# Embedding, first normalisations and first v product run between the columns of the edge placing; groups go from PSUM to their places by ScalarE

## The reference, cut to what matters

```
h = max(layernorm(x), 0)                      # the first normalisation
# L0: 4 blocks of conditioned norm, attention over edges, MLP
emb  = concat(sin(noise * freqs), cos(noise * freqs))
cond = silu(emb @ f_w1 + f_b1) @ f_w2 + f_b2   # one row of 16 per node
for i in range(4):
    y = norm(x) * (1 + cond @ s1_w[i] + s1_b[i]) + cond @ b1_w[i] + b1_b[i]
    q, k, v = y @ wq[i] + bq[i], y @ wk[i] + bk[i], y @ wv[i] + bv[i]   # 4 heads of 128
    scores = (q[src] * k[dst]).sum(-1)
    ... softmax over the edges of one src, sum of attn * v[dst], @ wo[i] + bo[i]
    x = x + ...          # then a second conditioned norm and a relu MLP
# then L1 (one SAGE-like layer), L2 (two relational layers), L3 (two SAGE layers)
```

## Time and profile before

| | |
|---|---|
| median of 3 runs | 3067.86 us (3063.8 to 3068.15) |
| the profiled execution | 3068.89 us |
| its span (first to last instruction) | 3067.1 us |
| mean granted clock of TensorE | 0.972 of full |
| busy in the span | PE 2871.9, DVE 2059.3, ACT 810.1, POOL 765.6 us |

### The profile page before, as it was taken

The page is one execution under the profiler, slowest core; times in us unless marked ns, Lnnn a source line. Parts: engine busy times, 40 slices in busy tenths (PEclk is TensorE's granted clock), DMA queues, the critical chain, the costliest instruction groups (busy, mean ns, idle before and its releaser), DMA issues.

```text
span 3067.1 us, 31231 instructions
## 1 busy us (share of the span) xinstructions
PE 2871.9 (94%) x11230; PEld 1810.2 (59%) x11230; DVE 2059.3 (67%) x3698; ACT 810.1 (26%) x1152; POOL 765.6 (25%) x701
## 2 busy tenths in 40 slices
PE   5878899999999999999999999999999999999999
PEld 1245556676556666556667555667645566556555
DVE  9999856786757776756777765778787876623211
ACT  1154442223212222221222321222322213213221
POOL 5732403343023334022334130334410000000000
PEclk9989999999999999999999999999999999999999
DMA  3000110000300000310000220000245244421001
GB/s 83 17 8 1 42 55 1 1 28 30 125 21 14 1 28 14 117 45 14 1 28 1 86 90 14 1 28 1 69 124 153 66 130 141 127 82 38 14 0 34
DMA packets 74679, 143.61 MB, mean 47 GB/s; under 512 B 11429, under 2 KB 11820, under 8 KB 74525
## 3 DMA queue, kind: packets, MB, share of 16 engines
q1 hardware_dynamic: 68988, 129.58, 13.6%
q0 software_dynamic: 5536, 12.03, 1.2%
HBM read 130.66 MB, written 10.92 MB: 46 GB/s over the span
## 4 chain that ended last, share of the span: by engine, by line
PE 69%; DVE 21%; issue 5%; ACT 3%; DVEq 1%; DMA 1%; POOL 0%; POOLq 0%; SPq 0%
PE ps L1547 14%; PE ps L1777 11%; PE ps L1806 10%; PE ps L1658 6%; PE ps L1751 4%; PE ps L1538 4%; DVE prob L1025 4%; DVE x L1015 3%; PE ps L1500 2%; PE ps L1798 2%; PE ps L1564 2%; PE ps L1647 2%; PE ps L1632 2%; DVE ps L971 2%; DVE onehot_src L896 2%
## 5 line engine op out<-in xcount | busy, mean ns | idle before, releaser
L703 POOL TENSOR_TENSOR pacc<-pacc,prob 125x628 f32<-125x628 f32 (+1 forms) x288 | 405.3, 1407 | 348.9 <-DVE prob L1044 348.9
L1547 PE MATMUL ps<-yT,w 128*128 128x416 f32 (+1 forms) x1152 | 442.5, 541 | 18.5 <-DVE qk_lo L962 11.6
L1658 PE MATMUL ps<-prob,big 125*128 125x314 f32 x1280 | 393.8, 430 | 14.0 <-DVE prob L1044 10.7
L1366 ACT ACTIVATE prob<-prob 125x628 f32<-125x628 f32 x320 | 233.0, 728 | 572.8 <-DVE prob L1025 572.8
L1806 PE MATMUL ps<-pieces,counts_r 125*125 125x512 f32 x1400 | 355.8, 409 | 0.0
L1547 PEld LDWEIGHTS ps<-yT,w 128*128 128x128 f32 x1152 | 229.0, 201 | 206.8 <-issue 195.5
L1044 DVE SCALAR_TENSOR_TENSOR prob<-prob,typed 125x628 f32<-125x628 f32 x320 | 260.3, 813 | 70.4 <-ACT prob L1366 68.2
L1806 PEld LDWEIGHTS ps<-pieces,counts_r 125*125 125x125 f32 x1400 | 259.1, 187 | 77.6 <-issue 17.4
L1647 PE MATMUL ps<-qk_hi 128*125 128x314 f32 x640 | 270.1, 422 | 11.2 <-DVE prob L1025 10.6
L1658 PEld LDWEIGHTS ps<-prob,big 125*128 125x128 f32 x1280 | 227.6, 190 | 81.0 <-DVE prob L1044 27.2
L1025 DVE TENSOR_TENSOR prob<-ps,shift 125x628 f32<-125x628 f32 x320 | 257.3, 804 | 4.4 <-PE ps L1649 3.7
(11 more groups left out here) (213 smaller groups left out, 4411.2 us busy)
## 6 DMA issues: line engine op xcount, KB each, us to landing
basis<-in_basis SPq DMA_DIRECT2D x160, 256.0 KB, 2.7
lite_ring<-in_basis SPq DMA_DIRECT2D x120, 256.0 KB, 2.6
w<-in_m_w SPq DMA_DIRECT2D x8, 1024.0 KB, 6.7
w<-in_wk SPq DMA_DIRECT2D x5, 1024.0 KB, 6.7
w<-in_wv SPq DMA_DIRECT2D x4, 1024.0 KB, 5.6
w<-in_wq SPq DMA_DIRECT2D x4, 1024.0 KB, 5.4
oT<-in_cw SPq DMA_DIRECT2D x8, 512.0 KB, 3.8
w<-in_wo SPq DMA_DIRECT2D x4, 1024.0 KB, 5.4
```

The source lines that it names most:

```text
L703: nc.gpsimd.tensor_tensor(pacc[:, c0:c0 + nn], pacc[:, c0:c0 + nn], prob[:, n % 3, p0:p0 + nn], ALU.add).then_inc(psum_done, 1)
L1366: A.activation(prob[:, n % 3, :], prob[:, n % 3, :], ACT.Exp, scale=DH ** -0.5).then_inc(exp_done, 1)
L1547: last = mm(lin_ps(job, 128, nn), weight[:, k, m * 128:(m + 1) * 128], lhs[:, k, c0:c0 + nn], start=(k == 0), stop=(k == KD - 1))
L1658: last = mm(o_halves[:, b, :], vrow[:, t, h * DH:(h + 1) * DH], prob[:, n % 3, b * QUARTER:(b + 1) * QUARTER], start=(t == 0), stop=(t == ...
```

## The change

It moves work of block 0 ahead and takes another engine for the copies.

1. VectorE computes the phases ahead of the columns, and between columns: a tile's statistics behind each of columns 2, 4, ... 20, the low parts of the norm's matrices behind 14, the silu behind 25, the shifts behind 27, low parts of cond behind 34, 39, 44. From column 46 on, behind every eighth, one step of block 0's norm: statistics of tile n, scale of tile n - 2, addition of the bias to v of tile n - 5. TensorE has the counterpart: the hidden layer, cond, and per step a turn, a scale product and a v product. GpSimd's powers go between its one-hots.
2. In a group ScalarE reads the sum twice from PSUM, once to `run` and once to its place in `typed`, whose register it loads itself; VectorE makes `carry`. GpSimd takes no part. TensorE waits for `bucket_placed` before it reuses PSUM.
3. The first tile stage has no v product; behind tiles 2, 4, 6 and 8 (`TAKE_AT`) it has one of the first four products of head 1.
4. SyncE's loads stand in another order: noise and the embedding's weights, then x and wv, then the norm's matrices, the other weights and `att`, `gate_rows` last.

```diff
-PREP = (10, 20, 30)
-COND_AT = (40, 43, 46)
+STATS_AT, POWERS_AT, SHIFTS_AT = 2, 25, 27
+LOW_AT, HIDDEN_AT, SILU_AT = 14, 10, 25
+COND_AT, COND_LOW_AT = (30, 35, 40), (34, 39, 44)
+NORM_AT, NORM_EVERY = 46, 8
+TAKE_AT = (2, 4, 6, 8)
...
@@ VectorE
+            def first_norm_step(n):
+                if n < T:
+                    dve.wait_ge(x0_ready, n + 1)
+                    tile_statistics(n)
+                if 1 <= n <= T:
+                    tile_shift(0, n - 1)
+                if 2 <= n < T + 2:
+                    tile_scale(0, n - 2)
+                if 5 <= n < T + 5:
+                    if n == 5:
+                        dve.wait_ge(blkc_in, 32)
+                    add_v(first, n - 5)
...
+            first_phases()
             for c in range(EC):
...
+                n, rest = divmod(c - NORM_AT, NORM_EVERY)
+                if rest == 0 and n >= 0:
+                    first_norm_step(n)
...
             for g in range(GROUPS):
...
+                if g:
+                    if g >= 3:
+                        dve.wait_ge(group_full, g - 2)
+                    V.tensor_scalar(carry[:, g % 2, :], ident16[:], same[0:P, g - 1:g], None, ALU.mult).then_inc(carry_ready, 1)
...
-                if g == PREP[0]:
-                    first_norm()
-                if g == PREP[2]:
-                    finish_silu()
@@ ScalarE
+            norm(0)
             for g in range(GROUPS):
+                place = act.value_load(placei[0:1, g:g + 1], min_val=0, max_val=PLACE + (T - 1) * N)
                 act.wait_ge(*((group_full, g) if g else (onehot_used, STEPS)))
-                if g >= RUNS:
-                    act.wait_ge(bucket_placed, g - RUNS + 1)
                 A.activation(run[:, g % RUNS, :], ps[0:P, (g % 2) * 1536:(g % 2) * 1536 + N], ACT.Copy).then_inc(run_ready, 1)
-                if g + 1 < GROUPS:
-                    A.activation(carry[:, (g + 1) % 2, :], ident16[:], ACT.Copy, scale=same[0:P, g:g + 1]).then_inc(carry_ready, 1)
+                if g:
+                    A.drain()
+                A.activation(typed[:].bitcast(F16)[:, bass.ds(place, N)], ps[0:P, (g % 2) * 1536:(g % 2) * 1536 + N],
+                             ACT.Copy).then_inc(bucket_placed, 1)
@@ GpSimd
             for c in range(EC):
...
+                t = (c - NORM_AT - 3) // NORM_EVERY
+                if (c - NORM_AT - 3) % NORM_EVERY == 0 and 0 <= t < T:
+                    tile_power(t)
...
-            for g in range(GROUPS):
-                pool.wait_ge(run_ready, g + 1)
-                place = pool.value_load(placei[0:1, g:g + 1], min_val=0, max_val=(PLACE + (T - 1) * N) // 2)
...
@@ TensorE
+            def first_norm_step(n):
...
+                if 3 <= n < T + 3:
+                    norm_turn(0, n - 3)
+                if 1 <= n <= T:
+                    norm_scale(0, n - 1)
+                if 4 <= n < T + 4:
+                    t = n - 4
+                    if t == 0:
+                        pe.wait_ge(w_in[0], 16)
+                    pe.wait_ge(turned_ready, t + 1)
+                    row_product(first["v"][t], yT, t, w[0])
...
             for g in range(GROUPS):
                 if g >= 2:
-                    pe.wait_ge(run_ready, g - 1)
+                    pe.wait_ge(bucket_placed, g - 1)
...
+                    project(0)
+                    turn_counts(0)
+                    projected(0)
+                    for t in range(T):
+                        if t + 1 < T:
+                            turn_counts(t + 1)
+                        max_scores(0, 2 * t)
+                        max_scores(0, 2 * t + 1)
+                        if t in TAKE_AT:
+                            n = TAKE_AT.index(t)
+                            col_product(g["proj"][1][n], yT, n % 3, w[1 + n // 3], 1)
```

More of the change, by code:

```diff
@@ L81, in max_row @@
             g["mrow"][h] = [w.take() for _ in range(3)]
+    if first:
+        g["v"] = [w.take() for _ in range(T)]
     project(0)
-    g["v"] = [w.take() for _ in range(T)]
+    if not first:
+        g["v"] = [w.take() for _ in range(T)]
     project(1, 0)
@@ new lines, in _ @@
+            A.activation(typed[:].bitcast(F32), zcol[0:P, :].to_broadcast([P, PLACE]), ACT.Copy)
+            A.drain()
+            act.wait_ge(emb_ready, 1)
+            A.activation(emb, turns, ACT.Sin, scale=6.2831850)
+            A.drain().then_inc(emb_ready, 1)
+            act.wait_ge(stage_in, 16)
+            A.activation(cw[:, 0:2, :], stage, ACT.Copy).then_inc(cw_hi, 1)
+            for (c0, nn), job in zip(COLS, hj):
+                act.wait_ge(lin_full, job.full)
+                A.activation(z[:, c0:c0 + nn], lin_ps(job, COND, nn), ACT.Identity, bias=fb1[:]).then_inc(lin_empty[job.slot], 1)
@@ L1521, in _ @@
[L1521 to L1532 removed]
+            first = plan_block(walk, True)
@@ new lines, in _ @@
+            pe.wait_ge(turned_ready, T)
+            for g in range(GROUPS):
+                if g >= 2:
+                    pe.wait_ge(bucket_placed, g - 1)
+                for j in range(STEPS):
+                    n = g * STEPS + j
+                    pe.wait_ge(onehot_ready, n + 1)
+                    for c0, nn in WIDE:
+                        last = mm(ps[0:P, (g % 2) * 1536 + c0:(g % 2) * 1536 + c0 + nn], onehot_dst[:, g % 2, j, :],
+                                  onehot_src[:, n % 4, c0:c0 + nn], start=(j == 0), stop=(g == 0 and j == STEPS - 1))
+                    last.then_inc(onehot_used, 1)
+                if g:
+                    pe.wait_ge(carry_ready, g)
+                    pe.wait_ge(run_ready, g)
+                    for c0, nn in WIDE:
+                        last = mm(ps[0:P, (g % 2) * 1536 + c0:(g % 2) * 1536 + c0 + nn], carry[:, g % 2, :],
+                                  run[:, (g - 1) % RUNS, c0:c0 + nn], start=False, stop=True)
+                    last.then_inc(group_full, 1)
@@ new lines, in _, with turn_counts @@
+            pe.wait_ge(bucket_placed, GROUPS)
+            def turn_counts(s):
+                if s:
+                    pe.wait_ge(crow_copied, s)
+                dst_ps = o_ps[0:P, :].bitcast(F16)
+                for t in range(T):
+                    if s == 0:
+                        pe.wait_ge(ct_ready, t + 1)
+                    c0 = t * (P + 1) if t < 8 else 1024 + (t - 8) * (P + 1)
+                    last = nc.tensor.transpose(dst_ps[:, c0:c0 + P], ct[:, t, s * P:(s + 1) * P], ident16[:])
+                last.then_inc(crow_ps_full, 1)
@@ L1567, in norm_tiles, with col_product @@
+            def col_product(job, lhs, chunk, weight, m):
+                c0, nn = COLS[chunk]
+                reuse(job)
+                for k in range(KD):
+                    last = mm(lin_ps(job, 128, nn), weight[:, k, m * 128:(m + 1) * 128], lhs[:, k, c0:c0 + nn],
+                              start=(k == 0), stop=(k == KD - 1))
+                last.then_inc(lin_full, 1)
             def norm_tiles(k, update, product):
```

436 lines of the change are left out of this document (210 added, 226 removed).

## The result

The changed kernel takes 3078.64 us (median of 7 runs, 3075.99 to 3081.62) against 3067.86 (7 runs, 3063.80 to 3068.66): a ratio of 1.0038, 95% interval 1.0027 to 1.0049. It is slower by 10.8 us. The forecast, 3068.5, is missed by 10.1; the range of 3056 to 3092 holds the time.

A forecast was written before the change was run, and what follows sets the result against it. VectorE was taken to bound the groups, and with GpSimd the columns. Stage ends summed to -1.2 us at the exponentials, taken as +0.6 for optimistic hand-offs: 3068.89 + 0.6 - 1.0 = 3068.5 us, range 3056 to 3092.

The forecast's parts named there:

- What bounds the kernel: Prologue: VectorE and GpSimd both full in the columns, VectorE leading in the groups, TensorE setting the pace of ten tiles.
- Columns: Placing of 160 edge columns: 54.5 us of moved VectorE work and 11 of waits added, 158.5 us in all.
- so about 0.9 us is uncovered, 10 times: 9: Norm steps between columns: TensorE's 5.1 to 5.3 us outlasts VectorE's step and four columns, 9 us over ten steps.
- Seam: Between columns and groups: GpSimd's 18.2 us of stacking and addition holds up the 6.8 us setup; 1.5 slips through, 23.5.
- Groups: The 59 groups: 2.77 us each with ScalarE copying twice and its register load hidden, 167.3 us in all.
- Products: Between groups and tiles: six products of 2.81 us and 1 us for their ends, 17.9 us.
- Tiles: First tile stage: four pairs of 9.3 us, two plain tiles, start and last maxima, 2 for a lower clock: 48.0 us.
- Tail: From the end of the tiles to attention's exponentials: 10.7 of 20.9 us stay once the four products have moved.
- Exposed load: Rival, groups: ScalarE's register load or a longer pause between copies is exposed; 3089 us, 3074 at half; chance 0.17.
- Slow TensorE in the columns: Rival: TensorE stays at 1.2 GHz in the columns, up to +45 us, 3089 at half; chance 0.18 with its mild form.
- mild form: Rival, columns: VectorE waits for ScalarE's xn or TensorE's scale behind the v product, +10 us, 3079; within the 0.18.
- Cheaper seam: Rival: the seam between columns and groups loses 8 to 12 us, or tile pairs are shorter; 3057 us, chance 0.25.

The follow-up runs named there:

- e1_pool_late: Changed kernel, with GpSimd's second stacking and addition of brow to x waiting for ScalarE's six high parts of head 0: 3067.67 us, ratio 0.9999 to before.
- e7_two_loads: Changed kernel with ScalarE's register load of the place doubled in every group: 3077.42 us, ratio 1.0028 to the kernel before.

## Why the prediction was off

- *What bounds the kernel.* Right.
- *Columns*, 158.5 predicted, 164.2 measured. The mechanism was right and its price was not. For a full step the terms hold: eight columns (4.65), the step's 2.63 and 0.9 uncovered give a period of 8.2, and 8.14 was measured. The step that failed: "so about 0.9 us is uncovered, 10 times: 9". It was 1.2 to 1.7 six times, and 1.45 to 2.8 in the last four steps, where VectorE's share of the step has shrunk to less than 1.3 us and covers less of TensorE's: 16.7 in all, 17.8 with the small pauses, instead of 9, and 2.5 instead of 2 for cond. The miss is only 5.7 because the other term was too high: 164.2 - 92.9 - 17.8 - 2.5 leaves 51.0 for the 54.5 of VectorE's own work. That is luck, and in the 51.0 are 1.1 us that I had not thought of: in the new order of loads the edge types, for which VectorE waits first, land at 6.0 us instead of 4.9 (5.3 to 6.0 in the nine kernels with that order, 4.9 in the two without). That the two makers of one-hots are equally long was seen, but not used; GpSimd's four take 2.42 where I had 2.3 for VectorE's, 0.1 us a period.
- *Seam*, 23.5 against 21.6. The mechanism was right and e1_pool_late shows it; 3.4 us slipped through (18.2 + 6.8 - 21.6), not 1.5. The Trainium skill, SBUF — State Buffer, section "SBUF: two separate sides", gave me a gap through which nothing slips. But it also names the VectorE operations that need the shared pair, those in a two-port mode or with two inputs in SBUF, and with that most rows agree: the casts and the tensor_scalar stand (10.19, 2.18, 2.33 us), the reduction and the copy out of PSUM don't (1.40, 0.65 us). `gcmp`, with two inputs in SBUF, took its own 1.40; there GpSimd's addition stood instead, 3.27 us for 1.89, which is 1.38 more. So one of the two stood for the other's whole length, as the section has it. It also lets the one go on that starts first, and by the recorded starts that was GpSimd, by 0.13 us; this part the row doesn't bear out.
- *Groups*, 167.3 against 167.4, to the rows: 2.77 predicted, 2.775 measured. The register load is hidden, as taken; e7_two_loads shows it. The Trainium skill, DMA: Bandwidth & Descriptors, section "Latency and other measured facts", has a floor of 600 ns for a tensor load. The trace has 278 ns for this one (median of 59, from 273), so here the floor doesn't hold; and it would cost nothing in this place, since two loads, 1.04 us with their checks, still fit under the copy.
- *Products*, 17.9 against 18.3: right.
- *Tiles*, 48.0 against 53.1, a term mis-sized, in two parts. "With hand-offs 9.3" has TensorE's part of a pair at 4.36 us (0.75, 0.8, 2.81); measured are 6.22 (1.32, 1.15, 3.75), with ScalarE's part as reckoned, so 11.08 for the pair and, for the next, 449.57 - 438.91 = 10.66. The 2 us put aside for a lower clock were too few. The landing of the counts, for which ScalarE is idle 2.10 us, was not in it at all.
- *Tail*, 10.7 against 12.6. The last two products take 7.60 us as before (7.56). What is longer is the row of maxima in front of them: its matmuls take 414 ns instead of 272, at a granted clock of 0.50 (459.6 to 462.7), and 1.95 us of them stand on the chain where before had 0.66. Some 0.4 us is no miss: the prediction counts the tail of before as 20.9 us, the table as 21.3.
- *Rivals.* Exposed load: fallen. Slow TensorE in the columns: fallen where it mattered, the v product takes 3.43 us there. Its mild form gave 3079, where the time came out, but by another wait than it named. Cheaper seam: by 1.9 us only.

The misses sum to 5.7 - 1.9 + 0.1 + 0.4 + 5.1 + 1.9 = 11.3, the whole distance of the exponentials from 460.9 to 472.2. The prediction has the exponentials of before at 462.1 and the table at 462.7, so the sum forecast -1.2 us and +9.5 came, a miss of 10.7. The time lies in the range because it had been opened to 3092 for an exposed load and slow columns, and neither of them came; what came, a dearer ring in the columns and slower pairs in the tiles, was in none of the rivals at its size.

## What to carry to other kernels

Work put between the items of a ring costs more than its own length as soon as one engine's share of it outlasts the ring: count the items in flight against the longest piece, for every engine that fills the ring and for the last steps too, in which the others have less to do meanwhile, and deepen the ring with the same edit. When work is moved ahead, look at what its engine has queued next: here 18 us of GpSimd work slid, without being touched, onto a setup that needed the port. A piece woven into a chain of waits in series is in series itself; put it where the chain already waits.

## What the hardware showed beyond that

Beside a GpSimd addition of 11 us a cast of 125 x 125 took 10.19 us instead of 0.23 and a tensor_scalar of 1250 f16 elements 9.68 instead of 0.49, while a VectorE operation with one input in PSUM and a memset kept their times; a float32 reduction kept its time beside the first addition of the stacking. GpSimd is held up in its turn: that addition took 3.27 us beside `gcmp`, 1.89 otherwise.

The prediction left open whether TensorE runs at its 1.2 GHz level in the columns. The same matmul of 472 columns answers it by its duration: 549 to 553 ns for all 160 in the kernel before; in the changed one 549 to 617 up to 117.7 us (one of 517), and 359 to 373 from 118.2 us on, behind the first turn of the norm and ahead of the first v product. I read that as the lower and the upper level; the granted clock in the windows says 1.00 in all of these stretches and doesn't show it.
